# Batch 0's feed-forward, norms and routing woven into batch 1's tiles, shared expert in halves, second residual on TensorE

## The reference, cut to what matters

```python
x = x + layernorm(block(layernorm(x)))      # x: [2, 2048, 128]
x = x + layernorm(moe(layernorm(x)))
# block(x): Performer attention with 16 heads of width 8, 32 random features a head
#   phi(u) = exp(u@omega.T - |u|^2/2 - max) / sqrt(32) + 1e-6      for q and k
#   kv = sum over the whole sequence of phi(k)^T v;  z = sum of phi(k)
#   out = phi(q) kv / (phi(q) z) @ wo
#   x = layernorm(x + out) * ln1_g + ln1_b
#   x = layernorm(x + gelu(x@w1 + b1)@w2 + b2) * ln2_g + ln2_b     hidden width 512
# moe(x): shared expert silu(x@w1.T)@w2.T for every row, hidden width 512, plus the
#   two best of 8 experts for each row, weighted by a softmax of their two logits
```

## Time and profile before

| | |
|---|---|
| time, median of 3 runs | 615.32 us (615.24 to 616.12) |
| the profiled execution's own time | 615.61 us |
| its span, first to last instruction | 613.9 us |
| tile loop, iterations 18 to 33 | 90.2 to 175.0 us of the span |
| pipeline | 175.0 to 422.6 us |
| expert blocks | 422.6 to 564.0 us |
| end | 564.0 to 613.9 us |

### The profile page before, as it was taken

The page is one execution under the profiler, slowest core; times in us unless marked ns, Lnnn a source line. Parts: engine busy times, 40 slices in busy tenths (PEclk is TensorE's granted clock), DMA queues, the critical chain, the costliest instruction groups (busy, mean ns, idle before and its releaser), DMA issues.

```text
span 613.9 us, 10584 instructions
## 1 busy us (share of the span) xinstructions
PE 472.9 (77%) x3392; PEld 363.1 (59%) x3392; DVE 322.8 (53%) x1322; ACT 236.3 (38%) x476; POOL 270.3 (44%) x376
## 2 busy tenths in 40 slices
PE   4799999999989976787856664667999999997000
PEld 3477767667646643565635443346999988897000
DVE  5887786678553668799955432300222232322273
ACT  3555444544543332323232332242444443542043
POOL 7200000110001446356888875510466556566593
PEclk9899999999989987957797786878999999999655
DMA  8910000000000000000010121334322222221631
GB/s 285 358 34 18 19 18 1 2 1 1 2 1 0 2 1 0 2 0 19 18 35 32 58 66 57 102 110 139 112 72 78 81 71 77 80 64 38 231 129 68
DMA packets 23220, 38.08 MB, mean 62 GB/s; under 512 B 4384, under 2 KB 14880, under 8 KB 22912
## 3 DMA queue, kind: packets, MB, share of 16 engines
q1 hardware_dynamic: 13248, 23.78, 12.1%
q0 software_dynamic: 4544, 9.45, 4.6%
q10 hardware_dynamic: 5376, 4.20, 2.0%
HBM read 21.74 MB, written 15.66 MB: 61 GB/s over the span
## 4 chain that ended last, share of the span: by engine, by line
PE 54%; POOL 15%; DVE 12%; another core or an unknown queue 7%; issue 5%; ACT 4%; DMA 2%; POOLq 0%; DVEq 0%; ACTq 0%; SPq 0%
PE pQKV L883 6%; POOL xs L504 5%; PE pF L601 4%; PE pPK L792 4%; PE pPK L599 3%; PE pPQ L883 3%; PE pKV L676 3%; PE pPK L600 3%; PE pF L705 3%; PE pPK L601 3%; PE pF L599 3%; PE pF L600 2%; DVE MID L1098 2%; PE pQKV L845 2%
## 5 line engine op out<-in xcount | busy, mean ns | idle before, releaser
L566 POOL DMA_INDIRECT ys<-MID,PQT x78 | 75.8, 972 | 25.7 <-issue 25.7
L444 POOL TENSOR_TENSOR ve<-mv,eps 128x4 f32<-128x4 f32 x40 | 8.2, 206 | 176.1 <-DVE mv L1091 176.0
L504 POOL DMA_INDIRECT xs<-PL,SLOT x64 | 62.5, 976 | 18.6 <-issue 18.6
L1404 DVE TENSOR_SCALAR MID<-pQKV,PQT 128x128 f32<-128x128 f32 x40 | 12.2, 346 | 74.5 <-remote 46.2
L599 PE MATMUL pPK<-XFH,E1H 128*128 128x512 f16 x32 | 15.2, 475 | 40.5 <-ACT HT L1015 23.0
L792 PE MATMUL pPK<-ATX,w_s 128*128 128x512 f32 x64 | 37.3, 720 | 9.7 <-ACT HT L995 8.8
L448 POOL TENSOR_TENSOR rs<-ve,halves 128x4 f32<-128x4 f32 x40 | 40.7, 1017 | 3.1
L883 PE MATMUL pQKV<-E,HT 128*128 x320 | 39.2, 276 | 1.7 <-ACT HT L1047 1.1
L437 POOL TENSOR_TENSOR held<-halves 128x1 f32<-128x1 f32 x47 | 9.3, 197 | 67.9 <-DVE MID L1404 58.2
L883 PEld LDWEIGHTS pQKV<-E,HT 128*128 128x128 f32 x320 | 37.3, 192 | 2.4 <-issue 2.2
L883 PE MATMUL pPQ<-E,HT 128*128 x304 | 37.3, 276 | 0.8 <-DVE MID L1404 0.8
(11 more groups left out here) (256 smaller groups left out, 1319.0 us busy)
## 6 DMA issues: line engine op xcount, KB each, us to landing
PQT<-xs SPq DMA_DIRECT2D x39, 132.0 KB
PQT<-in_ew1T SPq DMA_DIRECT2D x1, 2304.0 KB, 9.7
E<-in_ew2T SPq DMA_DIRECT2D x1, 2304.0 KB, 10.3
X<-in_x SPq DMA_DIRECT2D x8, 256.0 KB, 6.1
HT<-in_ew1T SPq DMA_DIRECT2D x8, 256.0 KB, 4.2
sh<-PK ACTq DMA_DIRECT2D x8, 256.0 KB
PQT<-sh SPq DMA_DIRECT2D x8, 256.0 KB, 4.2
PQT<-ys SPq DMA_DIRECT2D x4, 512.0 KB
```

Source lines behind the costliest of these rows:

```text
L504: eng.indirect_dma_start(xs, bass.IndirectOffsetOnAxis(SLOT[:, g, t, a:a + 1], 0), PL[:, g, t, a, :], None).then_inc(s_scat[g], 16)
L566: eng.indirect_dma_start(ys, bass.IndirectOffsetOnAxis(XS[q][:, t, ID_AT:ID_AT + 1].bitcast(U32), 0), Y[q][:, t, :], None).then_inc(s_ysc[ ...
```

## The change

Batch 0's work of pieces 5 to 21 moves out of the pipeline into iterations 22 to 33 of the tile loop (pipeline: 33 steps; group 0 never enters it, groups 1, 2 and 3 enter at pieces 19, 12 and 5, groups 4 to 7 at piece 0 two steps apart). To free PSUM banks for it, the tiles from 18 on use one bank for the raw key features (pPK[0]) and put the raw query features into pQKV, over q, k and v; and the list no longer looks ahead: a tile's bias is transposed and added in its own iteration. The second residual is no longer added by VectorE (L1265, L1267 and L1291 go) but by four TensorE products with the identity that open the down product's bank, from a copy X2T that ScalarE makes; norms 2 and 3 move from VectorE to ScalarE (`norm_act`), for which GpSimd makes minus mean times root (`neg_mean`, two small instructions). The shared expert comes in two halves at the end of each step, from step 13 on. In the first tiles the splits of five experts' weights come earlier, one a tile, and three instead of eight experts are loaded again.

```diff
+        STEPS = 33
+        SHARED = 13
+        FIRST = {GB - 3: 19, GB - 2: 12, GB - 1: 5}
+
+        def pipeline(stage, shared):
+
+            for s in range(STEPS):
+                for n in range(GB - 3, NG):
+                    stage(n, s + FIRST.get(n, -STAGGER * (n - GB)))
+                shared(*divmod(s - SHARED, 2))
+
+        def quarter(j):
+
+            return divmod(j - LEAD, T) if j >= LEAD else (None, None)
+
+        single = lambda j: j >= LEAD
+        pk_bank = lambda j: pPK[0] if single(j) else pPK[j % 2]
+        pq_bank = lambda j: pQKV if single(j) else pPQ
+        ff_bank = lambda n: pPK[1] if n < GB - 1 else pQKV
...
+                if j > LEAD:
+                    pe.wait_ge(s_mxq, j)
                 three(pQKV[:, 0:3 * D], xt(j), w(0, 3 * D)).then_inc(s_qkv, 1)
-                if j >= 2:
+                if j > LEAD:
+                    pe.wait_ge(s_ek, j)
+                elif j >= 2:
                     pe.wait_ge(s_ek, j - 1)
...
             def pq(j):
-                if j:
+                if single(j):
+                    pe.wait_ge(s_vx, j + 1)
+                    pe.wait_ge(s_sq, j + 1)
+                elif j:
                     pe.wait_ge(s_mxq, j)
...
+            def down(n):
+
+                bank = ff_bank(n)
+                pe.wait_ge(s_x1t, 2 * n + 2)
+                if n < GB - 1:
+                    pe.wait_ge(s_ge, (n + 1) * FC)
+                elif n == GB - 1:
+                    pe.wait_ge(s_mxq, 2 * NT)
+                else:
+                    pe.wait_ge(s_no[2], n)
+                for t in range(T):
+                    nc.tensor.matmul(bank[:, t * P:(t + 1) * P], X2T[:, t * P:(t + 1) * P], ident[:],
+                                     start=(t == 0), stop=False, skip_group_check=True)
+                pe.wait_ge(s_ge, (n + 1) * FC)
...
+            def shared(m, h):
+                if 1 <= m <= NG:
+                    shared_down(m - 1, h)
+                if 0 <= m < NG:
+                    shared_up(m, h)
...
+            for j in range(LEAD, 2 * NT + 2):
+                g, p = quarter(j)
+                tile = j < 2 * NT
+                if p == 0 and g >= 1:
+                    turn_n1(g - 1)
+                if p == 1:
+                    turn_den(g)
+                if p == 2:
+                    turn_recip(g)
+                if p == 3:
+                    attn_out(g)
+                if tile:
+                    qkv_pk(j)
+                elif j == 2 * NT:
+                    sum_kv(j - 1)
+                else:
+                    turn_kv(1)
+                if p == 1 and g >= 1:
+                    up(g - 1, 0)
+                if p == 2 and g >= 2:
+                    logits(g - 2)
+                if tile:
+                    pq(j)
+                if p == 0:
+                    num_den(g)
+                if p == 1 and g >= 1:
+                    up(g - 1, 1)
+                if p == 1 and g >= 2:
+                    turn_xf(g - 2)
+                if p == 1 and g >= 1:
+                    up(g - 1, 2)
+                if p == 2 and g >= 1:
+                    down(g - 1)
+                if p == 3:
+                    features_of(j // T - 1)
+                if p == 3 and g >= 2:
+                    count_rows(g - 2)
+                if tile:
+                    turn_bias(j)
+                    sum_kv(j - 1)
+                    bias_k(j)
+                if p == 1 and g >= 1:
+                    up(g - 1, 3)
+                if p == 0 and j // T + 1 < NG:
+                    turn_xn(j // T + 1)
...
+            def norm_act(j, n, src):
+                g = n % GB
+                act.wait_ge(s_nm[j - 2], n + 1)
+                for t in range(T):
+                    s = A(NY[n % 2][:, t * D:(t + 1) * D], src[:, t * D:(t + 1) * D], ACT.Identity,
+                          scale=rs[:, j, g, t:t + 1], bias=nm[:, j - 2, g, t:t + 1])
+                s.then_inc(s_no[j], 1)
...
+            def shared_out(m):
+                act.wait_ge(s_sd, m + 1)
+                if m >= 2:
+
+                    act.wait_ge(s_shst[m % 2], 16 * (m // 2))
+                A(SH[m % 2], pPQ[:].rearrange("p (c f) -> p c f", c=CH), ACT.Copy).then_inc(s_sh, 1)
```

More of the change, by code:

```diff
@@ L230, in build @@
         SH = [PK[:, q, :, 0:P] for q in range(2)]
-        HS = [[HT[:, c, :] for c in range(EC)], [MID[:, 0, :]] + list(parts(pq, *[GW] * (EC - 1)))]
+        HS = [list(parts(half[:, q * EC * GW:], *[GW] * EC)) for q in range(2)]
         OUT = [v[:, i, :] for v in (HT, XN) for i in range(4)]
@@ L797, in stage @@
[L797 to L801 removed]
+                    down(n)
                 if k == 15:
[L803 to L805 removed]
+                    turn_xf(n)
@@ L849, in _ @@
-            pipeline(stage)
+                    logits(n)
+                if k == 18:
+                    count_rows(n)
+            pipeline(stage, shared)
             banks = [pF[0], pF[1], pPK[0], pPK[1]]
@@ new lines, in gelu @@
+            def gelu(n, c):
+                bank = ff_bank(n) if n < GB - 1 else pPK[c % 2]
+                if c == 0:
+                    wait(act, s_dn, n)
+                act.wait_ge(s_up, n * FC + c + 1)
+                A(HT[:, c, :], bank[:], ACT.Gelu, bias=cols_s[:, 2 + c:3 + c]).then_inc(s_ge, 1)
+            def norm_act(j, n, src):
+                g = n % GB
+                act.wait_ge(s_nm[j - 2], n + 1)
+                for t in range(T):
+                    s = A(NY[n % 2][:, t * D:(t + 1) * D], src[:, t * D:(t + 1) * D], ACT.Identity,
+                          scale=rs[:, j, g, t:t + 1], bias=nm[:, j - 2, g, t:t + 1])
+                s.then_inc(s_no[j], 1)
@@ L1217, in res1, with norm1, stats2, stats3 @@
                 stats(1, n, XN[:, n])
-            v.memset(held[:, 0:1], 0.0).then_inc(s_batch, 1)
-            for j in range(2 * NT + 2):
-                g, piece = early(j)
+            def norm1(n):
+                if n == 0:
+                    dve.wait_ge(s_spare, 16 * 2)
+                wait(dve, s_nT, n)
+                norm(1, n, tiles(N1), XN[:, n])
+            def stats2(n):
+                dve.wait_ge(s_dn, n + 1)
+                stats(2, n, ff_bank(n))
+            def stats3(n):
+                hold(s_y2, n + 1, at=3)
+                stats(3, n, NY[n % 2])
```

759 lines of the change are left out of this document (440 added, 319 removed).

## The result

The changed kernel takes 644.55 us (median of 4 runs, 642.4 to 645.4) where the kernel before takes 615.41 on the same chip: ratio 1.0466, 95% interval 1.0439 to 1.0493. The forecast was 607 us, a gain. The profiled execution has a span of 642.8 us.

The account below looks back on a forecast made before the run. TensorE bounds iterations 18 to 33 and the expert blocks; in the pipeline nothing is full. Weave +54.2, splits +3, pipeline -67, lower clock +4, last store -2: -7.8 from 615.61 gives 607.8, as median 607; range 591 to 625.

Parts of the forecast that it names:

- the weave: Tile loop, iterations 18 to 33, with batch 0's work moved in: 139 us against 84.8, so +54.2.
- The splits ahead of it: Before iteration 18: five weight splits on VectorE, one a tile where it has little room, cost +3 us.
- The table loads: Tile loop: 12 new ScalarE table loads of 1.28 us, 9 of them on the chain.
- the rival of a dear switch: Tile loop, iterations 22 to 31: a table switch costs ScalarE twice its row, 11.5 us more, 619 us; chance 0.17.
- the long waits: Pipeline's end: ScalarE's shared copy waits long for its store, 9 us, expected once and not three times.
- The term of the pipeline: Pipeline after the tile loop: 181 us against 247.6, so -67.
- the rival that moves the work and no more: Pipeline: the long waits stay three, since the new order does not touch their cause; 615 us, chance 0.08.
- The four trains: Pipeline steps 20 to 27: four scatters of 10.1 us, 41 in all, GpSimd full, shared expert hidden beside it.
- steps 0 and 1: Pipeline's first steps: 9 us, where ScalarE's list starts with group 2's third norm.
- the cycle: Pipeline steps 8 to 14: down product, Gelus, norms 3 and 2 in turn, 13.5 us per two steps, lengthened to 17 and 14.2.
- The rival in which the clock falls in the weave: Tile loop: TensorE's 110 us of work at a granted 0.8 become 137, 10 more than taken; 618 us, chance 0.12.
- The 2 us from the last store beside the first load: Before the expert blocks: the last shared store lands beside the first block's load, -2 us.

Follow-up runs that it names:

- the scatters last: Changed kernel with GpSimd's scatters at the end of each pipeline step, behind roots and means: ratio 1.0394 alone, 0.9991 with a landing wait after every fourth scatter.
- the wait-cured kernel: Changed kernel in which GpSimd waits after every fourth scatter until it has landed: ratio 1.0170 to the kernel before, 629.2 us.

## Why the prediction was wrong

**Right: the weave.** 57.1 us for 54.2, 119 us of TensorE for 110. From kv product to kv product, groups g = 0, 1 and 2 took 28.8, 33.8 and 37.2 us for 28, 36 and 37; g = 3, to the pipeline's first, 40.3 for 38. The splits ahead of it cost 3.7 for 3. That the sum came out is partly luck. The table loads that I put at 9 x 1.28 = 11.5 us on the chain (9 where the 54 are split up) cost some 4 in all; the late signal inside the loop, which no term had, cost 4 (with the wait after every fourth scatter, the stretch from group 3's kv product to the second turn of kv takes 28.5 us for 32.7); so everything else took some 6 us more than priced, and no run says which wait. The loads are 15, as foreseen. The exp begins where a load ends:

```profile
137.10 1.28 ACT L1080 ACT_TABLE_LOAD   x1
138.39 0.60 ACT L1080 ACTIVATE PK<-pPK 128x512 f32<-128x512 f32 x1
```

so the rival of a dear switch, and with it the 2.66 us of the Trainium skill (ScalarE: Activation LUTs, "What ACT_TABLE_LOAD costs"), finds nothing here. The load's 1.28 us agree with the page, a drain on top does not show.

**The step that failed: the long waits.** The term of the pipeline took them from three to one, 32.5 us to 9, "since the copies stand three steps behind their stores". They are not for stores (eight buffers change nothing, the store looked at had landed 26 us before), so the new order could not remove them. They come with unbroken scatter trains, and the changed kernel has those as well: 11.9, 2.1 and 3.5 us in one place, 8.1 on VectorE, 5.5 again, and 8.6 in the loop. The earlier trace rows had shown it: VectorE was released with ScalarE though it waits for no store. The prediction said so and gave it 0.08, as the rival that moves the work and no more. The four trains took 55 us where 41 were forecast. An addition in every four scatters frees 18 us of the kernel before. In the changed one the wait after every fourth frees 18, and 25 with the scatters last (1.0394 to 0.9991). So the change didn't end the late signals, which the sum had booked as won, and it pays for them at least as much as the kernel before.

**Mis-sized: steps 0 and 1**, 21.7 us for 9. The prediction put group 2's scatter ahead of a root in a later cycle, and overlooked that group 1's stands ahead of the root of norm 4 at the very start, with VectorE, ScalarE's list and TensorE behind it. With the order turned the wait-cured kernel gains 7.3 us there. What is left, 15.7, is still 7 over the forecast; a table load of 1.28 us and products at half clock are in it, and their share wasn't measured.

The long waits and these first steps together are most of the miss: with the wait after every fourth scatter and the scatters last the changed kernel falls from 1.0466 to 0.9991, 29 of the 37 us between forecast and measurement. The other 8 aren't taken apart.

**Mis-sized: the cycle**, 16.1, 14.9 and 18.3 us where 17, 13.5 and 14.2 were forecast. The chain is as foreseen (down products wait 2.7 to 4.6 us for `norm_act`), but behind each wait the clock is lower (0.73 from 310.8 to 317.2), and residual and down products take 6.3, 7.4 and 6.8 us instead of 4.4:

```profile
310.84 2.02 PE L831 MATMUL pQKV<-ident,MID 128*128 128x128 f32 x8 [2.72 <-ACT MID L1125]
312.65 4.52 PE L836 MATMUL pQKV<-w_s,HT 128*128 128x128 f32 x32
```

The rival in which the clock falls in the weave did not come: it was 0.95 there, and fell in the pipeline instead (0.71 in steps 0 to 7). The 2 us from the last store beside the first load weren't won: from the last shared copy to the first block's is 3.3 us in both.

**What the change is worth.** It depends on what GpSimd does between the scatters: from 4.7% slower to 1.5% faster in the table above. Each kernel at the best that was tried, the changed one (0.9991) is 2.8% behind the one before (0.9714); that part of the 4.66% stays when both are treated, and the late signals and GpSimd's order account for the rest. By stages, with an addition in every four (the late signal inside the loop is still there): the weave costs 57 and the splits 4, and the pipeline to the first block's copy gives back 38 (175.0 to 407.0 in the one, 236.2 to 430.4 in the other). The work was put into a stretch where each tile's chain now runs through three engines. That this chain outweighs the gaps which the work left in the pipeline is read from these sums, no run isolates it. Not tried: the weave with a second bank for the key features; and in the changed kernel an addition behind batch 0's scatters too, or additions without the scatters last.

## What to carry to other kernels

A long wait must be checked against the moment at which its supposed cause ended; here the packets of the queue, and another engine released at the same instant, showed what the name of the semaphore hid. Where one engine issues a long train of indirect transfers, look whether others see TensorE's results late, and break the train. A cheap instruction can be enough: in the kernel before it gained 2.2% over a wait for landing (which stood behind batch 0's scatters too), in the changed one the two came out alike behind the loop. On an in-order engine, put what others wait for (here 1 us roots) ahead of what nobody waits for (5 us of scatters), unless that engine itself is the bound: the same order cost the kernel before 2% (1.0140 for 0.9931), where GpSimd is full.

## What the runs showed of the hardware

- Behind some five or more scatters of 128 rows issued 1.27 us apart, ScalarE and VectorE began 3 to 16 us late what TensorE had finished (in the train from 376.8 us of the changed kernel hand-offs were on time until 379.5, and late for what ended at 382.9). Most such waits ended 1.4 to 3 us after the train, some inside it (392.4 and 395.2 in the changed kernel). Gaps end it: 2.31 us between two starts once in four was enough, but for one hand-off 1.8 us late, 1.88 was not. At most four in flight or as many as come made no difference, and additions in the scatters' place delayed nothing. All late hand-offs looked at start at TensorE. By what path the scatters delay them stays open.
- TensorE ran at its lower clock behind waits in the pipeline (0.51 granted from 242.5 to 248.1 us of the changed kernel, behind one of 4.3 us, and 0.50 from 252.5 to 256.3, behind one of 4.5). Products that nobody reads raised it (0.84 for 0.60 over 21.5 us) and gained no time, part of them standing on the chain themselves; what the lower clock costs there stays open.
